# FFN weights quantised by two comparisons with half the scale, split over GpSimd and VectorE

## The reference

```
def _quant_weight(w):
    scale = jnp.mean(jnp.abs(w)) + EPS
    wq = jnp.clip(jnp.round(w / scale), -1.0, 1.0)
    return (wq, scale)
def _quant_act(x):
    s = jnp.max(jnp.abs(x), axis=-1, keepdims=True) / 127.0 + EPS
    xq = jnp.clip(jnp.round(x / s), -128.0, 127.0)
    return (xq, s)
def _qlinear(x, w):
    wq, ws = _quant_weight(w)
    xq, xs = _quant_act(x)
    return jnp.einsum('bsi,oi->bso', xq, wq) * xs * ws
...
gate = jax.nn.silu(_qlinear(x, w_gate))
up = _qlinear(x, w_up)
return _qlinear(gate * up, w_down)
```

## Time and profile before

| | |
|---|---|
| time, median of 3 runs (lowest to highest) | 2201.02 us (2199.70 to 2203.93) |
| the profiled execution, its own time | 2198.97 us |
| its span | 2197.3 us |
| busy, share of the span | PE 88%, PEld 69%, DVE 64%, ACT 43%, POOL 24% |
| the weight block | 1115.5 to 1193.3 us, 3.5% of the span |

### The profile page before, as it was taken

One profiled execution on the slowest core, in us unless ns is written; L12 is line 12 of the kernel. 1 busy time (PEld: TensorE's weight loads), 2 busy tenths in 40 slices (PEclk: granted clock), 3 DMA queues, 4 the chain that ended last, 5 costly groups with the idle time before them and its releaser, 6 DMA issues. The chain is left out here.

```text
span 2197.3 us, 33249 instructions
## 1 busy us (share of the span) xinstructions
PE 1923.5 (88%) x11722; PEld 1506.8 (69%) x11722; DVE 1413.1 (64%) x2748; ACT 948.6 (43%) x1971; POOL 521.1 (24%) x477
## 2 busy tenths in 40 slices
PE   1899999999599999999933899799976989999997
PEld 1677787777367787777722555566643879999996
DVE  3766666676666666667677777467664535666663
ACT  1333344433243334443356333355533425666663
POOL 3211001110321101011011200133222354555553
PEclk9999999999699999999965999899997999999999
DMA  5201001100320010110042000000004147777784
GB/s 136 75 1 37 37 37 37 37 1 1 77 75 14 25 37 37 37 37 1 1 202 90 0 0 0 1 1 1 1 1 159 45 126 179 231 233 232 233 241 96
DMA packets 39528, 154.58 MB, mean 70 GB/s; under 512 B 5472, under 2 KB 12848, under 8 KB 29050
## 3 DMA queue, kind: packets, MB, share of 16 engines
q1 hardware_dynamic: 27170, 128.39, 16.6%
q0 software_dynamic: 11408, 23.37, 5.9%
q10 hardware_dynamic: 840, 1.36, 0.2%
HBM read 132.59 MB, written 20.51 MB: 70 GB/s over the span
## 5 line engine op out<-in xcount | busy, mean ns | idle before, releaser
L608 DVE TENSOR_TENSOR la_q_roped<-banks,la_rope_q 128x400 f32<-128x400 f32 x384 | 198.0, 567 | 45.7 <-PE banks L400 28.7
L555 ACT ACTIVATE la_probs<-banks,la_minus_max 100x361 f32<-100x361 f32 x256 | 144.4, 564 | 157.9 <-DVE la_minus_max L643 157.9
L1772 DVE TENSOR_TENSOR ex_weights_low<-ex_raw_weights,ex_weights_high 128x2048 fp32r<-128x2048 f32 x60 | 137.5, 2292 | 56.4 <-ACT ex_weights_high L1667 56.4
L643 DVE TENSOR_REDUCE la_minus_max<-banks 100x1 f32<-100x361 f32 x256 | 135.6, 530 | 59.0 <-PE banks L426 52.2
L343 POOL TENSOR_TENSOR la_wq_high<-la_weights,zero 128x1024 fp32r<-128x1024 f32 x14 | 26.5, 1892 | 608.2 <-PE banks L372 608.2
L435 PEld LDWEIGHTS banks<-identity,la_probs 100*121 100x121 f32 x768 | 113.5, 184 | 64.3 <-DVE la_probs L650 29.7
L446 PE MATMUL banks<-la_probs_t,la_kv_rows 121*128 121x200 f32 x768 | 151.3, 333 | 0.0
L925 PE MATMUL banks<-qf_sign_weights,qf_x_quant_t 128*100 128x512 bf16 x512 | 122.2, 389 | 29.5 <-DVE qf_hidden L1006 15.3
L573 ACT COPY la_probs_t<-banks 121x300 f32<-121x300 f32 x256 | 105.7, 413 | 96.8 <-PE banks L435 96.8
L435 PE MATMUL banks<-identity,la_probs 100*121 100x100 f32 x768 | 125.6, 272 | 16.0 <-DVE la_probs L650 14.5
L400 PE MATMUL banks<-la_q_roped,la_weights 128*64 128x400 f32 x768 | 139.6, 505 | 0.0
(11 more groups left out here) (314 smaller groups left out, 5331.7 us busy)
## 6 DMA issues: line engine op xcount, KB each, us to landing
ex_raw_weights<-w_exp SPq DMA_DIRECT2D x60, 1024.0 KB, 5.0
la_weights<-w_pack SPq DMA_DIRECT2D x16, 1984.0 KB, 7.9
qf_raw_weights<-w_ffn SPq DMA_DIRECT2D x2, 4096.0 KB, 21.4
qf_raw_weights<-w_ffn SPq DMA_DIRECT2D x2, 2048.0 KB, 7.4
out<-ex_block_out POOLq DMA_DIRECT2D x13, 256.0 KB, 4.4
residual<-x SPq DMA_DIRECT2D x1, 3200.0 KB
normed_rows<-ex_xn SPq DMA_DIRECT2D x16, 200.0 KB
out<-residual SPq DMA_DIRECT2D x4, 800.0 KB
```

The costliest lines, as they stand in the source:

```text
L555: act.activation(prob[:, s % 4, 0:L], ps[0:S, s % 2, 0:L], ACT.Exp, bias=nmax[:, s % 4:s % 4 + 1], accum_out=sums[:, s % 4:s % 4 + 1]).the ...
L608: dve.tensor_tensor(roped[:, h, v, c, :].rearrange("p (b s) -> p b s", b=GB), ps[:, B_BANKS[k % 2], 0:NT].rearrange("p (b s) -> p b s", b=GB),
L643: dve.tensor_reduce(nmax[:, s % 4:s % 4 + 1], ps[0:S, s % 2, 0:L], AX.X, ALU.max, negate=True).then_inc(s_max, 1)
L1772: dve.tensor_tensor(wl[:, m, :], raw[:, m, :], wh[:, m, :].bitcast(F32), ALU.subtract).then_inc(w_low[m], 1)
```

## The change

The quantised weight is computed in another way: it is 1 where w > scale/2, -1 where w < -scale/2, else 0, that is (w > t) - (w < -t) with t = scale/2. `inverse` becomes `threshold`, which writes t and -t in place of the reciprocal. ACT's `weight_round` and DVE's clip and subtraction go. For each half there are now two instructions that read `raw` unchanged: a comparison w < -t, written into `wq` as 1 or 0, and DVE's SCALAR_TENSOR_TENSOR, (w > t) minus what stands in `wq`, in place. The comparison of half 0 is made by POOL (`negative`), that of half 1 by DVE. DVE takes half 1 first, so that half is also reloaded first. The lists of ACT, PE and DVE are rearranged.

```
+                def negative(m):
+                    pool.wait_ge(w_thr, 2 * m + 2)
+                    pool.tensor_scalar(wq[:, m, 0:HALF], raw[:, m % 2, 0:HALF], nthr[:, m:m + 1], None,
+                                       ALU.is_lt).then_inc(w_neg, 1)
...
                 for g in range(B // XG):
+                    if g == 2:
+                        negative(0)
+                        negative(1)
...
+                negative(2)
...
-                def weight_round(m):
...
                 weight_sum(0)
-                weight_round(0)
+                weight_sum(1)
                 x_round(0)
                 x_round(1)
-                weight_sum(1)
-                weight_round(1)
+                weight_sum(2)
                 x_round(2)
                 x_round(3)
-                weight_sum(2)
-                weight_round(2)
...
+                def threshold(m):
                     dve.wait_ge(w_tot, m + 1)
...
+                    dve.tensor_scalar(thr[:, k], wscale[:, k], 0.5, None, ALU.mult).then_inc(w_thr, 1)
+                    dve.tensor_scalar(nthr[:, k], wscale[:, k], -0.5, None, ALU.mult).then_inc(w_thr, 1)
 
                 def quantise(m):
...
+                    k = slice(m, m + 1)
+                    dve.wait_ge(w_thr, 2 * m + 2)
+                    for p in (1, 0):
+                        hs = slice(p * HALF, (p + 1) * HALF)
+                        if p:
+                            dve.tensor_scalar(wq[:, m, hs], raw[:, m % 2, hs], nthr[:, k], None,
+                                              ALU.is_lt).then_inc(w_neg2, 1)
+                            dve.wait_ge(w_neg2, m + 1)
+                        else:
+                            dve.wait_ge(w_neg, m + 1)
+                        dve.scalar_tensor_tensor(out=wq[:, m, hs], in0=raw[:, m % 2, hs], scalar=thr[:, k],
+                                                 in1=wq[:, m, hs], op0=ALU.is_gt,
+                                                 op1=ALU.subtract).then_inc(w_done, 1)
```

More of the change, by code:

```diff
@@ L704, in quantised_ffn @@
         xqt = sb("x_quant_t", [128, KC, B * S], BF16)
-        wsum, wscale, winv = sb("w_abs_sums", [128, 3]), sb("w_scale", [128, 3]), sb("w_inverse", [128, 3])
+        wsum, wscale = sb("w_abs_sums", [128, 3]), sb("w_scale", [128, 3])
+        thr, nthr = sb("w_threshold", [128, 3]), sb("w_minus_threshold", [128, 3])
         ones = sb("ones", [128, 128])
@@ L740, in _ @@
                     sp.dma_start(raw[:, m, :], w_ffn[m]).then_inc(loaded[m], 16)
-                for p in range(2):
-                    sp.wait_ge(w_done, p + 1)
+                for k, p in enumerate((1, 0)):
+                    sp.wait_ge(w_done, k + 1)
                     hs = slice(p * HALF, (p + 1) * HALF)
@@ L846, in _ @@
                 x_scales(1)
-                inverse(0)
+                threshold(0)
                 quantise(0)
+                threshold(1)
                 x_quantise(0)
                 x_quantise(1)
+                quantise(1)
                 x_turned(0)
                 x_turned(1)
-                inverse(1)
+                threshold(2)
                 x_scales(2)
                 x_scales(3)
-                quantise(1)
+                quantise(2)
                 x_quantise(2)
@@ L860, in _ @@
                 x_turned(3)
-                inverse(2)
-                quantise(2)
                 dve.tensor_scalar(gscale[:], xscale[:], wscale[0:S, GATE:GATE + 1], None, ALU.mult).then_inc(scales, 1)
@@ L886, in _ @@
                 total(0)
+                total(1)
                 turn_x(0)
                 turn_x(1)
-                total(1)
+                total(2)
                 turn_x(2)
                 turn_x(3)
-                total(2)
         staging.close()
```

18 lines of the change are left out of this document (4 added, 14 removed).

## The result

The changed kernel takes 2225.16 us (median of 4 runs, 2224.49 to 2226.78), the kernel before 2202.47 in the runs beside them (4 runs, 2199.70 to 2206.08). The ratio is 1.0103, with an interval of 1.0086 to 1.0121. That is slower by 1%, clear of the noise and as forecast in direction, but by 22.7 us where 10.7 were forecast, and above the range. The profiled execution took 2225.39 us, with a span of 2223.7.

What follows compares the result with a forecast made beforehand. DVE's list, from gate's scale to its last weight-block instruction (56.2 us), was taken to set the block's end. Eleven steps, with POOL and DVE taking turns, summed to 66.9: +10.7 on the 2201.02 median gives 2211.7 us, range 2206 to 2222.

Steps and rivals of the forecast that it cites:

- 1, 3: thresholds of gate and up: DVE in the weight block: three small threshold instructions for gate and the same for up, 0.45 us each.
- 2: quantise gate: DVE's comparison 2.3, POOL's comparison 4.7, two SCALAR_TENSOR_TENSORs of 4.43 and 0.1 handing over, run in turn: 16.0 us.
- 4: two `x_quantise`: After up's threshold: two `x_quantise`, 2.36 us, with POOL's comparison of 4.7 getting in between or right behind: 7.1 us.
- 5: quantise up: DVE's 11.2 us of work on up, plus 2.0 for two or three POOL normalisations getting in between: 13.2 us.
- 6, 7: copies; total and threshold of down: DVE copies the first eight transposed tiles, 3.6 us, then makes down's total and threshold, 0.3 + 0.45.
- 8: `x_scales` of the last groups: DVE's scales of the last two groups, 5.2 us, plus 2.5 for a tiny TENSOR_SCALAR held by POOL's comparison: 7.7 us.
- 9: quantise down: DVE's comparison and two SCALAR_TENSOR_TENSORs on down, POOL being done: 11.2 us.
- 10, 11: `x_quantise`, copies, scales: End of DVE's block: `x_quantise` and copies of the last two groups, 6.0 us, then three small scales, 0.5.
- Comparison on POOL: Pricing of POOL's 128x4096 comparison from its TENSOR_SCALAR of 512 columns at 0.75 us: 4.7 us, bounds 3.75 and 8.9.
- My upper bound: Highest price considered for POOL's 128x4096 comparison, at the two-input rate of 4.518 us for 2048 columns: 8.9 us.
- POOL compares slowly: Rival: POOL's comparison runs at the two-input rate, 8.9 us; +23.3 us in all, 2224.3; chance 0.09.
- P: Time of one POOL comparison of 128x4096, made once for each of three matrices; taken as 4.7 us.

Runs made afterwards that it cites:

- the run with a pause: Changed kernel, with DVE made to wait on a semaphore for its second `x_quantise` before it starts the comparison of up; measured 2227.61 us.

## Why the prediction was wrong

The direction, the place and the mechanism (POOL's time lands on DVE's list) held; one term was far too small. By my own steps along DVE's list, in us:

| step | forecast | measured |
|---|---|---|
| 1, 3: thresholds of gate and up | 0.9 | 0.7 |
| 2: quantise gate | 16.0 | 19.7 |
| 4: two `x_quantise` | 7.1 | 2.3 |
| 5: quantise up | 13.2 | 19.6 |
| 6, 7: copies; total and threshold of down | 4.35 | 4.0 |
| 8: `x_scales` of the last groups | 7.7 | 15.1 |
| 9: quantise down | 11.2 | 11.2 |
| 10, 11: `x_quantise`, copies, scales | 6.5 | 6.35 |
| sum | 66.9 | 78.9 |

- **The step that failed** is "Comparison on POOL", and in it the sentence "I take 4.7 as the same kind of instruction". The row taken was the normalisation of the earlier trace rows, a TENSOR_SCALAR that multiplies and adds. Same opcode, another form: multiply-and-add takes 3.75 us at this size, one operation alone 10.6, comparison and multiplication 14.0. My upper bound, the rate of two true inputs in the earlier trace rows (8.9), did not hold it either: I took reading a second tensor for the worst that POOL can do. The rival "POOL compares slowly", which had 0.09, is what happened in kind. That its 2224.3 lies so near the 2225.16 measured is luck: it had P at 8.9 and not 10.5, 4.8 too little over the three, and my sum counts 5.3 too much elsewhere (below). The Trainium skill (GPSIMD Engine Reference, Performance pitfalls for Q7 kernels) gave 7.1 or 3.7 us by my estimate; its figures are for loops in kernels written for that engine, and the built-in instruction took 10.6, so they did not carry over. The Trainium skill (GPSIMD Engine Reference, Engine selection) also calls elementwise work with one input on that engine roughly line-rate; the runs do not bear that out for a single operation, with 10.6 us on POOL for 2.35 on DVE.
- **That POOL's time lands on DVE's list** was right: 15.5 us less on POOL is 15.5 us less in the list (half the columns), 10.3 more is 8.6 more (two operations), 20.6 less is 17.1 less (multiply-and-add), and no comparison on POOL is 19.1 less. In the second and third of these, what is missing is the early start of two SCALAR_TENSOR_TENSORs.
- **P three times.** With P = 10.5 my sum would give 28.1 over before, 5.3 too much. 1.9 of it lie in each of steps 2 and 5: the SCALAR_TENSOR_TENSOR begins about 1.9 us before POOL's instruction has ended. 2.0 lie in the normalisations of step 5: none gets in ahead of DVE there, they are held themselves (12.67 us for eight in place of 6.0). Against these 5.8 stand 1.6 too little in step 8: the held normalisations put off POOL's third comparison to 1186.10, so that only 0.5 us of it ran beside the reduction and not 2.3. The other steps together are 1.1 shorter than in my sum.
- **Step 4** had POOL in between two `x_quantise` or right behind them. It gets in at neither place, and P falls once into step 5 instead: this POOL instruction got its turn only where DVE paused, as the run with a pause shows.
- **Step 8** had the right instruction, the tiny one behind the reduction, held for P minus the reduction's rest: 9.9 in place of 2.5. Of the 7.4 between them, 5.8 are P and 1.6 the late start just told.
- **SCALAR_TENSOR_TENSOR** at 4.43, from the TENSOR_TENSOR of the earlier trace rows, measured 4.48. **ACT and the reloads** were no limit, as said: ACT waits 15.4 us for the reload and its sum ends at 1173.9, ten before DVE asks for it.
- **Two readings** in the prediction are a little off and change no term. DVE's waits for PE in the earlier trace rows add up to 4.6 us, not some 3. And the held TENSOR_TENSOR of the earlier trace rows did move before POOL had finished: 47.14 + 1.09 - 0.56 = 47.67, 0.15 ahead of POOL's end at 47.82.

After the block nothing new is seen: the profiled execution of after is longer by 26.4 us of span, 22.8 of them in the list, 1.2 ahead of it and the rest behind it, while the medians differ by 22.7. Why POOL is quick in the one form and slow in the other three is not shown by these runs; that its program for that pair is a special one would fit, and is only argued. A multiplication and addition with a constant, and other pairs with two scalars from memory, were not run.

## What to carry to other kernels

Price an instruction of POOL by a row with the same operations and the same kinds of scalars, not by one with the same opcode; where there is none, measure that form by itself before work is moved there, for the bounds can lie outside what the trace has. And where POOL and DVE take turns, work handed to POOL saves DVE its own short time and costs it POOL's: here 2.35 us given away came back as 8 to 10. The room that was free lay on ACT, and it was small: 1.9 us of DVE's list. POOL, as idle, had none.

## What the hardware showed that I had not expected

- POOL's TENSOR_SCALAR on 128 x 4096 float32: multiply and add, both scalars from memory, 3.75 us; a multiplication or a comparison alone 10.6 (2.53 ns a column, 0.24 us fixed; the same into bfloat16 and float32); comparison and multiplication 14.0.
- A SCALAR_TENSOR_TENSOR on two SBUF inputs begins before a slow POOL instruction has ended, by a time that does not go with the length. This is worked out, on the assumption that once free it takes its usual 4.48: in the changed kernel it begins at 1140.81 + 13.01 - 4.48 = 1149.34, from its longest duration in the row below, and POOL ends at 1151.26: 1.92 us. With half the columns it is 1.93, with two operations 2.79, with multiply-and-add 0.21. A one-input TENSOR_SCALAR waits for all but the last 0.2 us: in the run with a pause 1160.03 + 12.50 - 2.35 = 1170.18, against POOL's end at 1170.38. That POOL has read its last numbers by then would fit, but no run shows it.

```profile
L823 DVE SCALAR_TENSOR_TENSOR qf_sign_weights<-qf_raw_weights,qf_w_threshold,qf_sign_weights x6: 4472/4480/13007, 1140.8 to 1206.2; 128x4096 bf16<-128x4096 f32 x6
```

- A POOL MEMSET, 3.51 us, holds a one-input TENSOR_SCALAR of DVE (5.68 for 2.35) and leaves a SCALAR_TENSOR_TENSOR alone (4.48). It also got in between two one-input TENSOR_SCALARs of DVE with no pause between them, which POOL's comparison did not.
